# A gated block on one core: shorter routing, two weight loads and the biases moved in SyncE's queue, scale products moved to ScalarE

## What is computed

```
def bit_linear(x, w, b):
    gamma_x = clip(max(abs(x), axis=-1), 1e-05, None)
    scale_x = 127.0 / gamma_x
    x_dq = clip(round(x * scale_x), -128.0, 127.0) / scale_x
    gamma_w = clip(mean(abs(w)), 1e-05, None)
    w_dq = clip(round(w / gamma_w), -1.0, 1.0) * gamma_w
    return einsum('bsd,hd->bsh', x_dq, w_dq) + b

expert_ids = minimum(clip(token_ids, 0, 24999) // 6250, 3)
h = layernorm(x)
for e in range(4):
    g = silu(h @ W[e].T);  u = h @ W[e].T;  y = (g * u) @ W[e].T
    out = where(expert_ids == e, y, out)
x = x + tanh(g_xattn) * out
h = layernorm(x)
ffn = bit_linear(silu(bit_linear(h, gate_w, gate_b)) * bit_linear(h, val_w, val_b), out_w, out_b)
x = x + tanh(g_ffn) * ffn
```

## Time and profile before

| | |
|---|---|
| median of 3 runs | 312.35 us (312.32 to 313.3) |
| profiled execution | 312.77 us, span from first to last instruction 311.0 us |
| TensorE matmul busy | 292.2 us, 94% |
| VectorE busy | 261.6 us, 84% |
| GpSimd busy | 237.2 us, 76% |
| ScalarE busy | 216.9 us, 70% |
| DMA | 49.61 MB, mean 160 GB/s |

### The profile page before, as it was taken

One profiled execution on the slowest core, in us unless ns is written; L12 is line 12 of the kernel. 1 busy time (PEld: TensorE's weight loads), 2 busy tenths in 40 slices (PEclk: granted clock), 3 DMA queues, 4 the chain that ended last, 5 costly groups with the idle time before them and its releaser, 6 DMA issues.

```text
span 311.0 us, 5271 instructions
## 1 busy us (share of the span) xinstructions
PE 292.2 (94%) x1406; PEld 138.2 (44%) x1407; DVE 261.6 (84%) x496; ACT 216.9 (70%) x274; POOL 237.2 (76%) x260
## 2 busy tenths in 40 slices
PE   0999999999999999999889999999999999999984
PEld 0444555554544455444334444444444444444431
DVE  5898978878778886789998999999898889887871
ACT  3959586867768666777986796668866786666610
POOL 4546764788887878947678799998989887977752
PEclk9999999999999999999999999999999999999999
DMA  7676888848998880933044535764444434453064
GB/s 259 218 263 242 279 256 295 312 118 290 297 278 178 242 262 35 326 91 89 32 89 79 115 73 118 121 150 89 111 115 110 92 73 81 109 113 74 34 124 145
DMA packets 60997, 49.61 MB, mean 160 GB/s; under 512 B 53231, under 2 KB 53231, under 8 KB 58672
## 3 DMA queue, kind: packets, MB, share of 16 engines
q1 hardware_dynamic: 56416, 35.96, 46.4%
q0 software_dynamic: 4560, 13.40, 12.4%
HBM read 28.35 MB, written 10.00 MB: 123 GB/s over the span
## 4 chain that ended last, share of the span: by engine, by line
PE 68%; DMA 12%; DVE 9%; ACT 5%; issue 3%; POOL 2%; DVEq 0%; POOLq 0%; ACTq 0%
PE banks L617 17%; PE banks L690 17%; PE banks L699 16%; PE banks L714 15%; DMA tern<-h_sb 5%; DMA raw<-in_ctx 2%; DMA raw<-raw 2%; PE banks L624 1%; POOL w_both L474 1%; DVE raw L1163 1%; DVE raw L1168 1%; DMA xg<-in_x,gather_at 1%; DMA xg<-raw 1%; PE banks L594 1%; DVE gu_sb L1063 1%
## 5 line engine op out<-in xcount | busy, mean ns | idle before, releaser
L617 PE MATMUL banks<-w_both,turned 128*128 x348 | 80.2, 379 | 1.6 <-ACT turned L825 1.0
L474 POOL TENSOR_TENSOR w_both<-raw 128x1024 f32<-128x1024 f32 (+1 forms) x32 | 75.0, 2345 | 8.6 <-DVE raw L1163 7.7
L903 ACT ACTIVATE w_both<-w_both,magic,raw 128x1024 f32 (+1 forms) x31 | 38.2, 1234 | 36.0 <-DVE raw L1182 36.0
L714 PE MATMUL banks<-tern,xg 128*128 128x512 bf16 x256 | 59.9, 379 | 2.2 <-DMA xg<-raw 0.8
L699 PE MATMUL banks<-tern,raw 128*128 128x512 bf16 x256 | 60.5, 379 | 1.3 <-DVE raw L1155 1.3
L690 PE MATMUL banks<-tern,raw 128*128 128x512 bf16 x256 | 60.5, 379 | 0.6 <-DVE raw L1163 0.4
L617 PEld LDWEIGHTS banks<-w_both,turned 128*128 128x128 f16 x348 | 34.0, 98 | 39.3 <-issue 5.0
L1155 DVE SCALAR_TENSOR_TENSOR raw<-banks,raw 128x1024 f32<-128x1024 f32 x32 | 40.8, 1276 | 5.0 <-issue 4.4
L1163 DVE SCALAR_TENSOR_TENSOR raw<-banks,raw 128x1024 f32<-128x1024 f32 x32 | 40.9, 1278 | 4.0 <-PE banks L699 4.0
L1168 DVE TENSOR_REDUCE raw<-w_both 128x1 f32<-128x1024 f32 x32 | 38.8, 1211 | 3.2 <-POOL w_both L474 3.1
L714 PEld LDWEIGHTS banks<-tern,xg 128*128 (+1 forms) x256 | 24.8, 98 | 33.2 <-DMA xg<-raw 1.7
(11 more groups left out here) (126 smaller groups left out, 406.1 us busy)
## 6 DMA issues: line engine op xcount, KB each, us to landing
raw<-in_ctx SPq DMA_DIRECT2D x4, 1024.0 KB, 7.1
raw<-in_L_ffn_gate_w SPq DMA_DIRECT2D x4, 1024.0 KB, 6.8
raw<-in_L_ffn_val_w SPq DMA_DIRECT2D x4, 1024.0 KB, 7.2
raw<-in_L_ffn_out_w SPq DMA_DIRECT2D x4, 1024.0 KB, 7.7
raw<-x_low SPq DMA_DIRECT2D x8, 257.5 KB, 3.5
raw<-x_high SPq DMA_DIRECT2D x8, 257.5 KB, 3.4
raw<-in_L_ffn_gate_b SPq DMA_DIRECT2D x1, 1024.0 KB, 4.9
raw<-in_L_ffn_val_b SPq DMA_DIRECT2D x1, 1024.0 KB, 8.9
```

Source lines behind the costliest of these rows:

```text
L474: nc.gpsimd.tensor_tensor(z[:, t % 2, 2 * D * c:2 * D * c + width], g_sb[:, c, 0:width], v_sb[:, c, 0:width], ALU.mult).then_inc(z_made, 1)
L617: last = nc.tensor.matmul(acc[:, :], a[:, k * P:(k + 1) * P], flat(w[:, bass.ds(e4 + k, 1), :]), start=(k == 0 and i == 0), stop=(k == KD ...
L714: last = nc.tensor.matmul(to, flat(ziT[:, bass.ds(t % 2, 1), k, :]), tern[:, 2 * G + k, :], start=(k == order[0] * G // 2), stop=(k == (or ...
L903: nc.scalar.activation(zq[:, a:b], flat(z[:, bass.ds(t % 2, 1), a:b]), ACT.Identity, scale=flat(sc[:, bass.ds(t, 1), 12:13]), bias=magic[: ...
```

## The change

It has these parts:

- Routing. The compares read the int32 tokens directly instead of an f32 copy, and two of the masks come straight from a compare. The two additions that make the experts' bases become one scan. The multiplication by the row's number (`iota_id`) moves from `unit_hot` into `row_hot`, as a second operation of each of its 16 instructions.
- SyncE. Loads 8 and 9 stand ahead of the first transpose of h, behind a wait for gather 10; loads 10 and 11 each move two transposes up. The biases wait for 12 signs instead of 16.
- ScalarE. `w_copy(5)` stands in front of `w_scale(7)`. One new instruction behind each `x_round` makes both x scale products at once, and one behind each second `z_round` makes the z scale product; VectorE's three are gone.
- The floor 1e-5 of z is a 2049th column of z, written once by GpSimd and read by the second half's maximum; the maximum of both halves and the division by 127 are one instruction.

```diff
@@ SyncE
+            gathers_landed(10)
+            load_weights(8)
+            load_weights(9)
 
             for i, j in enumerate(H_DMA[:-2]):
                 turn_h(j)
-                if 8 + i < 12:
-                    load_weights(8 + i)
+                if 10 + i < 12:
+                    load_weights(10 + i)
...
-            sp.wait_ge(signed, G)
+            sp.wait_ge(signed, bias_frees)
             sp.dma_start(bias_g, gate_b.partition_broadcast(P)).then_inc(bias_loaded, 16)
@@ GpSimd
             for c in range(HOT_DVE, COLS):
-                nc.gpsimd.tensor_scalar(row_hot[:, c, :], iota_minus, minus_row[:, c:c + 1], None, ALU.is_equal).then_inc(hot_pool, 1)
+                nc.gpsimd.tensor_scalar(row_hot[:, c, :], iota_minus, minus_row[:, c:c + 1], iota_id[:, c:c + 1],
+                                        ALU.is_equal, ALU.mult).then_inc(hot_pool, 1)
...
+                    nc.gpsimd.memset(z[:, :, H:H + 1], 1e-5).then_inc(z_floor, 1)
                     z_pair(0, 0)
@@ ScalarE
                     w_high(7)
+                    w_copy(5)
                     w_scale(7)
-                    w_copy(5)
...
                 nc.scalar.activation(xq, xn, ACT.Identity, scale=flat(sc[:, bass.ds(t, 1), 2:3]),
                                      bias=magic[:, 0:1]).then_inc(xq_made, 1)
+                nc.scalar.activation(flat(sc[:, bass.ds(t, 1), 3:5]), gam[:, 0:2], ACT.Copy,
+                                     scale=flat(sc[:, bass.ds(t, 1), 1:2])).then_inc(xs2_made, 1)
...
+            def out_scale(t):
+                act.wait_ge(zs_made, t + 1)
+                nc.scalar.activation(flat(sc[:, bass.ds(t, 1), 13:14]), flat(sc[:, bass.ds(t, 1), 11:12]), ACT.Copy,
+                                     scale=out_gam[:, 0:1]).then_inc(zs2_made, 1)
@@ VectorE
-            then(v.tensor_copy(tokf, tok[:, :]))
             for k in range(1, E):
-                last = v.tensor_scalar(ge[:, k - 1, :], tokf, float(PER_EXPERT * k), None, ALU.is_ge)
-            then(last)
-            v.tensor_scalar(mask[:, 0:COLS, 0], ge[:, 0, :], -1.0, 1.0, ALU.mult, ALU.add)
+                v.tensor_scalar(ge[:, k - 1, :], tok[:, :], float(PER_EXPERT * k), None, ALU.is_ge)
+            v.tensor_scalar(mask[:, 0:COLS, E - 1], tok[:, :], float(PER_EXPERT * (E - 1)), None, ALU.is_ge)
+            then(v.tensor_scalar(mask[:, 0:COLS, 0], tok[:, :], float(PER_EXPERT), None, ALU.is_lt))
...
-            for k in range(2, E):
-                then(v.tensor_tensor(base[:, k:k + 1], base[:, k - 1:k], ceiled[:, k - 1:k], ALU.add))
+            then(v.tensor_tensor_scan(base[:, 1:E], ceiled[:, 0:E - 1], ceiled[:, 0:E - 1], 0.0, ALU.add, ALU.max))
...
-            then(v.tensor_tensor(unit_hot[:, 0, :, :], iota_raised.unsqueeze(1).broadcast_to([P, COLS, UNITS]),
-                                 unit_a.unsqueeze(2).broadcast_to([P, COLS, UNITS]), ALU.is_equal))
-            v.tensor_tensor(unit_hot[:, 1, :, :], unit_hot[:, 0, :, :],
-                            iota_id.unsqueeze(2).broadcast_to([P, COLS, UNITS]), ALU.mult).then_inc(unit_hot_made, 1)
+            v.tensor_tensor(unit_hot[:, :, :], iota_raised.unsqueeze(1).broadcast_to([P, COLS, UNITS]),
+                            unit_a.unsqueeze(2).broadcast_to([P, COLS, UNITS]), ALU.is_equal).then_inc(unit_hot_made, 1)
...
-                v.tensor_scalar(col(t, 3), gam[:, 0:1], col(t, 1), None, ALU.mult).then_inc(xs2_made, 1)
-                v.tensor_scalar(col(t, 4), gam[:, 1:2], col(t, 1), None, ALU.mult).then_inc(xs2_made, 1)
...
-                v.tensor_reduce(col(t, 5 + c), z[:, t % 2, 2 * D * c:2 * D * (c + 1)], AX.X, ALU.max,
+                if t == 0 and c == 1:
+                    dve.wait_ge(z_floor, 1)
+                v.tensor_reduce(col(t, 5 + c), z[:, t % 2, 2 * D * c:2 * D * (c + 1) + c], AX.X, ALU.max,
                                 apply_absolute_value=True).then_inc(zmax_made, 1)
...
-                v.tensor_scalar(col(t, 9), col(t, 5), col(t, 6), 1e-5, ALU.max, ALU.max).then_inc(z_step, 1)
-
-            def z_gamma(t):
-                dve.wait_ge(z_step, 2 * t + 1)
-                v.tensor_scalar(col(t, 11), col(t, 9), 1 / QMAX, None, ALU.mult).then_inc(z_step, 1)
+                v.tensor_scalar(col(t, 11), col(t, 5), col(t, 6), 1 / QMAX, ALU.max, ALU.mult).then_inc(z_step, 1)
...
-                v.tensor_scalar(col(t, 13), col(t, 11), out_gam[:, 0:1], None, ALU.mult).then_inc(zs2_made, 1)
```

27 lines of the change are left out of this document (15 added, 12 removed).

## The result

The changed kernel takes 311.5 us (median of 20 runs, 308.9 to 313.55) against 313.19 for the kernel before (20 runs beside it, 311.84 to 317.56): ratio 0.9935, interval 0.9913 to 0.9957. Two later comparisons gave 0.9911 [0.9879, 0.9944] and 0.9919 [0.9886, 0.9951]. The three say 2.0 to 2.8 us less, 2.5 on the mean; 3.6 were forecast. The forecast's 308.75 was counted from a median of three runs, 312.35; the median of 20 is 0.84 higher, and that much of the distance to 311.5 is the base and no term of the sum.

What follows compares the result with a forecast made beforehand. Bound by a chain of waits: other engines and loads until 31 us, then mostly TensorE, so VectorE savings count only in places. Terms 0.8 + 0.3 + 0.7 + 0.1 + 1.5 + 0.2 = 3.6 gave 308.75 us (307.8 to 309.8).

Steps and rivals of the forecast that it cites:

- A: Routing ahead of the first gather: fewer VectorE instructions win 0.75 us, taken as 0.8.
- B: w_copy(5) ahead of w_scale(7) on ScalarE: TensorE's wait at 31.01 us goes, 0.3 us won (0 to 0.6).
- C: Loads 8 and 9 ahead of the h transposes: 1.9 us given back less 1.2 lost, 0.7 won.
- D: Biases at the twelfth sign and x scales on ScalarE: 0.1 us won (-0.4 to 0.3).
- E: Start of the feed-forward part: less VectorE work shortens TensorE's four waits, 1.5 us won (0.5 to 2.4).
- F: Tail: z_gamma of the last tile goes, 0.2 us won on the path (0.1 to 0.35).
- The 5.65: Landing time in us of the x transpose behind the biases, used to price the first h transpose behind the loads.
- R1: First h transpose lands at 73 or later, slots 9 to 11 stretch: C = -1.5, 311.0 us; chance 0.15.
- R3: Routing: int32 compares are slow, A = 0.8 - 1.6, 310.4 us; chance 0.08.
- R4: Start of feed-forward part: GpSimd's z products are the limit, not VectorE; E = 0.5, 309.8 us; chance 0.12.
- R5: Slower than before: h transposes 9 to 11 each wait for a whole load; C = -6, 315.4 us; chance 0.04.
- R2: Early loads pay in full, gathers and scatters get quicker, all 2.7 us come back: 306.9 us; chance 0.14.

Runs made afterwards that it cites:

- start alone without the fold: Kernel before with only the shorter routing (row_hot in one operation as before) and w_copy(5) ahead of w_scale(7): 312.07 us, ratio 0.9962.

## Why the prediction was off

The direction was right; the 3.6 us were 2.5 (2.0 in the first comparison). The terms, as forecast and as the runs have them; a number that comes from ratios is uncertain by some 1.2 us to either side:

| term | forecast | measured | from |
|---|---|---|---|
| A, B start | 1.1 | 1.2 - 0.2 | start alone without the fold, 0.9962; the fold, by rows |
| C loads | 0.7 | -1.2 to -0.1 | undone, 0.988 against 0.9919; alone, 1.0005; rows of the first pair, -0.3 |
| D biases | 0.1 | 1.1 to 1.4 | alone 0.9964, undone 0.9963 |
| E feed-forward | 1.5 | 1.2 | rows, 159.56 to 158.37 |
| F tail | 0.2 | -0.5 | rows, tail 15.0 to 15.3 without the gap, 15.5 to 15.8 with it |

With C at -1.2 the sum is 1.2 - 0.2 - 1.2 + 1.1 + 1.2 - 0.5 = 1.6, with -0.1 it is 2.7; the measured 2.5 lies between, near the upper end.

**C is the step that failed**: it priced gather 11 at nothing. The forecast has the gather fly "between" the loads and then counts one loss, at the first transpose ("it lands at 72.7 instead of 70.3", "I count 1.2 us lost there"), against "I give back 1.9". In the profiled pair the transpose came out much as counted: it landed at 73.2, and slot 9 was 1.1 longer. What came back was 1.4 in slots 10 to 12 and 0.6 in slots 13 to 18, 1.9 together. But the gather landed 7.7 us behind its issue instead of 3.6, VectorE waited 1.08 for it, TensorE 1.23 for VectorE, and slot 8 was 1.2 longer. The sum for this pair is a loss of 0.3 instead of a gain of 0.7. The four other profiles with load 8 issued from 61.0 on also have a long slot 8 and a long slot 9, in other sizes; in three of them VectorE waits for the gather, in one ScalarE is late. Where load 8 was issued before 60 there is neither the wait for the gather nor a wait of TensorE near 72. That the late landing of the gather comes from the loads is shown by the seven profiles with before's order, 3.4 to 3.7 in all; why it is 4.9 in one execution and 8.3 in another stays open.

The 5.65 was taken from the transpose behind the biases. Ring order, which the forecast weighed in a sentence apart, gave 72.9, as near to 73.2 as one profile can tell. By the Trainium skill (DMA: Bandwidth & Descriptors, section "Queues, rings and completion order") each DMA engine consumes one issuer's ring in order; the profiles agree, with the transpose 0.6 to 3.7 us behind load 9 and never ahead of it. Rival R1 (C = -1.5) got 0.15. It has about the size of C that undoing the loads gives, but not the mechanism: of slots 9 to 11 only slot 9 stretched in the profiled pair (7.00, 6.08, 5.78 against 5.94, 5.76, 6.26), and the quiet slots did pay. That the forecast's 1.9 came back so nearly is in part luck: slots 9 to 12, 25.19 in the profile of before, took 23.5 to 25.4 in the seven profiles with that order of loads.

**F failed** through a cost that no row of before could show: the 0.47 gap depends on the count of VectorE instructions. Contention behind it adds to the loss: VectorE's half then starts second and takes 0.81 us more. The 0.2 that was forecast is there (0.45 from the first scale step to the rounding, 0.64 before), but without the gap the rounding runs beside a GpSimd product and takes 1.15 instead of 0.97, so even then the tail is no shorter.

**D was too small**, in the other direction. The forecast read from the profile that TensorE "only waited 0.15 us or so". But the transpose landed at 133.22 and TensorE's first product began at 133.26, as the table of stretches adds up: the chain had no slack, so each later landing counts in full, and 46 of 101 executions of before beside these runs were over 313.5. The profiled one was of the shorter ones (312.77).

**A**: the compares were right to be harmless (R3 fell), the CAST's 0.56 belonged to the CAST (the upper end, 0.4 more), and "I take nothing" for row_hot's second operation was wrong: 0.73, outside the bound of 0.4, more than the product it saved. By rows A is 0.45 instead of 0.8. **B** was right that the wait at 31 goes, and too small. **E** held: waits of 1.28 against the 0.9 forecast, and R4 (0.5) fell. R5 fell: with this order of loads no transpose of h took over 6.7. R2 fell.

## What to carry to other kernels

Ahead of a small urgent transfer, count the bytes queued in the same ring to their end, and ask when the wait in front of them ends in a late execution: with the bulk issued at 53 to 55 us instead of 59 to 63 the transpose landed in 3.1 to 3.9. Then go through every other transfer that flies beside the bulk, also from other engines' queues, and price its landing too; the one that cost TensorE its longest wait here was the gather. A transfer that lands just as its reader starts is a risk on one side, and one profile shows none of it: look at the spread of the single times before you price it. Folding a step into an instruction that runs 13 times pays only if the added operation is cheaper than a thirteenth of that step.
